# SSM front of a four-layer kernel: SiLU from the activation table, loop bodies ordered chunk by chunk

## What is computed

```
xr, gate = split(x @ W_in.T, 2)
xr = xr + t_emb[:, None, :]
xc = causal_conv(xr, W_conv, 4 taps) + b_conv
xc = silu(xc)
mu, var = xc.mean(-1), xc.var(-1)
xn = (xc - mu) / sqrt(var + 1e-05) * ln_g + ln_b
Bm, Cm, dt = split(xn @ W_xproj.T, 3)
dt = tanh(dt @ W_dt.T + b_dt) * 0.01
Ad = 1.0 + dt * -tanh(A_log)
Bd = Bm * minimum(norm(xn), 1.0)
h = clip(h * ad + bd * xt, -10, 10); y_t = c_t . h       (scan over the 64 tokens)
out = (y + D * xn) * silu(gate) @ W_out.T
```

## Time and profile before

| | us |
|---|---|
| median of 3 runs | 2034.54 (2029.61 to 2037.28) |
| the profiled execution, its own time | 2042.08 |
| its span in the profile | 2040.3 |
| busy in the span: PE, DVE, ACT, POOL | 1783.1, 1706.3, 1327.3, 658.3 |

### The profile page before, as it was taken

The page is one execution under the profiler, slowest core; times in us unless marked ns, Lnnn a source line. Parts: engine busy times, 40 slices in busy tenths (PEclk is TensorE's granted clock), DMA queues, the critical chain, the costliest instruction groups (busy, mean ns, idle before and its releaser), DMA issues.

```text
span 2040.3 us, 46458 instructions
## 1 busy us (share of the span) xinstructions
PE 1783.1 (87%) x15152; PEld 853.0 (42%) x15152; DVE 1706.3 (84%) x2508; ACT 1327.3 (65%) x2180; POOL 658.3 (32%) x592
## 2 busy tenths in 40 slices
PE   7899898998988787788998997987787889899978
PEld 5555455555544545442222223444454322222234
DVE  4778878787776898989999996668888899999965
ACT  4545445454443778698998992048776899899910
POOL 0233223332222011434765660001014356656500
PEclk9999999999998898979999999999998899999999
DMA  3000000000000333354554746712333545546477
GB/s 145 2 2 0 1 2 28 2 1 0 1 2 32 121 110 138 109 180 135 175 160 123 248 145 212 219 50 104 129 129 118 173 138 173 159 155 225 145 220 270
DMA packets 127179, 228.29 MB, mean 112 GB/s; under 512 B 36084, under 2 KB 61812, under 8 KB 118004
## 3 DMA queue, kind: packets, MB, share of 16 engines
q1 hardware_dynamic: 127064, 226.80, 34.1%
HBM read 143.40 MB, written 83.36 MB: 111 GB/s over the span
## 4 chain that ended last, share of the span: by engine, by line
PE 57%; DVE 18%; ACT 11%; issue 7%; DMA 4%; SPq 2%; DVEq 0%; ACTq 0%; POOL 0%; POOLq 0%
PE PS L1237 12%; PE PS L1254 12%; PE PS L1095 9%; PE PS L881 8%; DMA yt<-y_d 3%; DVE q L1669 3%; ACT ex L653 3%; DVE ex L1371 3%; PE PS L1257 3%; PE PS L1304 2%; PE PS L1148 2%; PE PS L947 2%; DVE sm L1377 2%; DVE mx L1367 2%; DVE z L1557 2%
## 5 line engine op out<-in xcount | busy, mean ns | idle before, releaser
L866 ACT ACTIVATE R<-q,Ast 128x512 f32<-128x512 f32 x1024 | 637.7, 709 | 42.3 <-DVE q L1669 29.6
L1669 DVE SCALAR_TENSOR_TENSOR q<-R,PS 128x512 f32<-128x512 f32 x1008 | 612.0, 705 | 20.4 <-PE PS L1237 10.1
L548 POOL TENSOR_TENSOR Uw<-Ub,rowmask 96x512 bf16<-96x512 bf16 x256 | 338.9, 1357 | 193.9 <-PE PS L1237 181.3
L1237 PE MATMUL PS<-xq,Uw 97*128 97x512 bf16 x1024 | 323.7, 394 | 53.4 <-DVE q L1669 39.3
L1254 PE MATMUL PS<-q,Wy 128*32 128x512 f32 x2016 | 284.7, 618 | 0.8 <-DVE q L1669 0.7
L539 POOL TENSOR_TENSOR xlo<-xr,xmi 128x512 bf16<-128x512 f32 x64 | 72.3, 1161 | 529.3 <-ACT xmi L791 529.3
L1237 PEld LDWEIGHTS PS<-xq,Uw 97*128 97x128 bf16 x1024 | 85.7, 97 | 366.6 <-DVE q L1669 321.2
L1095 PE MATMUL PS<-X,Win 128*128 (+1 forms) x512 | 232.0, 603 | 4.3 <-DVEq L1501 2.9
L881 PE MATMUL PS<-xn,Wl 128*128 128x512 f32 x384 | 185.4, 614 | 25.8 <-DVE xm L1347 19.0
L505 POOL TENSOR_TENSOR ex<-ex,rs 128x1024 f32<-128x1024 f32 x32 | 94.1, 2941 | 206.1 <-DVE rs L1380 206.1
L649 ACT ACTIVATE pT<-PS 128x512 f32<-128x512 f32 x128 | 75.3, 596 | 119.1 <-PE PS L947 118.9
(11 more groups left out here) (151 smaller groups left out, 2744.5 us busy)
## 6 DMA issues: line engine op xcount, KB each, us to landing
xq<-xpart_d SPq DMA_DIRECT2D x384, 192.0 KB
sg_d<-sg SPq DMA_DIRECT2D x16, 1024.0 KB, 4.2
xn_d<-z SPq DMA_DIRECT2D x16, 1024.0 KB, 4.0
y_d<-ys SPq DMA_DIRECT2D x64, 256.0 KB, 3.9
xnp<-xn_d SPq DMA_DIRECT2D x16, 1024.0 KB, 6.6
sgp<-sg_d SPq DMA_DIRECT2D x16, 1024.0 KB, 9.1
yt<-y_d SPq DMA_DIRECT2D x32, 512.0 KB, 10.0
xpart_d<-xh SPq DMA_DIRECT2D x16, 512.0 KB, 2.9
```

Of the source, the lines that this page charges most:

```text
L548: pl.tensor_tensor(Uw[0:XROWS, h, w, :, :, :], Ub[0:XROWS, w, 0:N, ds(s0, CH)].rearrange("p n t -> p t n").unsqueeze(2).broadcast_to([XROW ...
L866: act.activation(R[:, w, :], q[:, t % 2, w, :], ACT.Relu, scale=Ast[:, h, w, t:t + 1], bias=CLIP).then_inc(ac_r, 1)
L1237: pe.matmul(PS[:, w, :], Uw[0:KROWS, h, w, t, :, :].rearrange("p b n -> p (b n)"), xq[0:KROWS, hb, w, s8 % XT, :], start=True, stop=True). ...
L1669: v.scalar_tensor_tensor(out=q[:, s8 % 2, w, :], in0=R[:, w, :], scalar=2 * CLIP, in1=PS[:, w, :], op0=ALU.min, op1=ALU.subtract).then_inc ...
```

## The change

```diff
-LN_EXP_SET = 6
+LN_EXP_SET, SILU_TANH_SET = 6, 18
...
+            def silu_set():
+
+                act.add_instruction(mybir.InstLoadActFuncSet(name=nc.get_next_instruction_name(), act_func_set_id=SILU_TANH_SET))
...
+                silu_set()
                 act.activation(tA[:, :], dtp[:, 1:2], ACT.Tanh).then_inc(tA_r, 1)
...
-                def gate_tanh(n):
-                    for m in range(DC):
-                        act.wait_ge(g_mm, n * DC + m + 1)
-                        act.wait_ge(z_r, n * DC + m + 1)
-                        act.activation(th[:, m, :], PS[:, m, :], ACT.Tanh, scale=0.5).then_inc(sgt_r, 1)
-
-                def conv_tanh(n):
-                    for m in range(DC):
-                        act.wait_ge(cv_r, n * (3 * DC) + 2 * DC + m + 1)
-                        act.activation(th[:, m, :], acc[:, m, :], ACT.Tanh, scale=0.5).then_inc(th_r, 1)
...
+                def conv_silu(n, m):
+                    act.wait_ge(cv_r[2], n * DC + m + 1)
+                    act.activation(zs[:, m, :], acc[:, m, :], ACT.Silu).then_inc(z_r, 1)
+
+                def gate_silu(n, m):
+                    act.wait_ge(sg_st, n * 16 + 16)
+                    act.wait_ge(g_mm, n * DC + m + 1)
+                    act.activation(sg[:, m, :], PS[:, m, :], ACT.Silu).then_inc(sg_r, 1)
...
                 def decay_in(it):
+                    act.wait_ge(xd_mm, it + 1)
+                    act.activation(dts[:, :], PS[:, 6, 2 * P:3 * P], ACT.Copy).then_inc(dts_r, 1)
+
+                def minus_c(it):
                     act.wait_ge(xw_mm, it + 1)
-                    act.activation(dts[:, :], PS[:, 6, 2 * P:3 * P], ACT.Copy).then_inc(dts_r, 1)
                     act.wait_ge(pick_st, it * PICK + PICK)
                     act.activation(Cn[:, :], PS[:, 6, P:2 * P], ACT.Copy, scale=-1.0).then_inc(C_r, 1)
...
                 def body(it):
-                    logarithm_set()
-                    tap(it + 1)
                     log_std(it, 4)
-                    for m in range(DC):
-                        shifted(it, m)
-                    for m in range(DC):
-                        squared(it, m)
-                    conv_tanh(it + 1)
-                    gate_tanh(it + 1)
+                    silu_set()
+                    tap(it + 1, 0)
+                    tap(it + 1, 1)
+                    tap(it + 1, 2)
+                    gate_silu(it + 1, 0)
+                    shifted(it, 0)
+                    shifted(it, 1)
+                    squared(it, 0)
+                    gate_silu(it + 1, 1)
+                    shifted(it, 2)
+                    shifted(it, 3)
+                    tap(it + 1, 3)
+                    gate_silu(it + 1, 2)
+                    squared(it, 1)
+                    squared(it, 2)
                     decay_in(it)
+                    conv_silu(it + 1, 0)
+                    squared(it, 3)
+                    high_part(it, 0, 0)
                     decay_tanh(it, PS[:, 4, 0:P])
+                    conv_silu(it + 1, 1)
+                    high_part(it, 1, 1)
+                    gate_silu(it + 1, 3)
+                    conv_silu(it + 1, 2)
+                    conv_silu(it + 1, 3)
                     logarithm_set()
                     log_norm(it)
-                    for k in range(TT):
-                        high_part(it, k, k)
                     mean(it + 1)
-                    for k in range(TT):
-                        middle_part(it, k)
-                    squares(it + 1)
-
-                tap(l * G)
-                conv_tanh(l * G)
-                gate_tanh(l * G)
+                    minus_c(it)
+                    high_part(it, 2, 2)
+                    middle_part(it, 0)
+                    high_part(it, 3, 3)
+                    middle_part(it, 1)
+                    for m in range(DC):
+                        square(it + 1, m)
+                    middle_part(it, 2)
+                    middle_part(it, 3)
+
+                for m in range(DC):
+                    tap(l * G, m)
+                for m in range(DC):
+                    conv_silu(l * G, m)
+                for m in range(DC):
+                    gate_silu(l * G, m)
                 mean(l * G)
-                squares(l * G)
+                logarithm_set()
+                for m in range(DC):
+                    square(l * G, m)
                 with act.Fori(0, G - 1) as g:
                     body(l * G + g)
-                logarithm_set()
                 log_std(l * G + G - 1, 6)
...
+                def x_in_proj(it, g, m):
+                    pe.wait_ge(xr1_r, it * TT + m + 1)
+                    into(it + 1, g + 1, m, xr_mm)
+
+                def turned_x(it, k):
+                    pe.wait_ge(sg_r, (it + 1) * DC + k + 1)
+                    turn_x(it, k, k)
+
                 def body(it, g):
-                    for m in range(DC):
-                        pe.wait_ge(sg_r, it * DC + m + 1)
-                        pe.wait_ge(xr1_r, it * TT + m + 1)
-                        into(it + 1, g + 1, m, xr_mm)
-                    variance(it, 4)
-                    gates(it + 1, g + 1, 0, DC - 1)
+                    x_in_proj(it, g, 0)
+                    variance(it, 0, 4)
+                    x_in_proj(it, g, 1)
+                    variance(it, 1, 4)
+                    variance(it, 2, 4)
+                    variance(it, 3, 4)
+                    x_in_proj(it, g, 2)
+                    gate_in(it + 1, g + 1, 0)
                     pe.wait_ge(zr_r, it * 3 + 3)
                     spread_out(5, zr, zb_mm)
-                    gates(it + 1, g + 1, DC - 1, DC)
-                    project_part(it, 2)
-                    project_part(it, 0)
-                    project_part(it, 1, xw_mm)
-                    norm(it)
-                    for k in range(TT):
-                        pe.wait_ge(sg_r, (it + 1) * DC + k + 1)
-                        turn_x(it, k, k)
-                        if k == 0:
-                            decay(it, PS[:, 4, 0:P])
+                    gate_in(it + 1, g + 1, 1)
+                    x_in_proj(it, g, 3)
+                    gate_in(it + 1, g + 1, 2)
+                    norm(it, 0)
+                    project_part(it, 2, xd_mm)
+                    turned_x(it, 0)
+                    turned_x(it, 1)
+                    decay(it, PS[:, 4, 0:P])
+                    gate_in(it + 1, g + 1, 3)
                     pe.wait_ge(dtt_r, it + 1)
-                    mean(it + 1)
+                    mean(it + 1, 0)
+                    norm(it, 1)
+                    mean(it + 1, 1)
+                    norm(it, 2)
+                    turned_x(it, 2)
+                    norm(it, 3)
+                    mean(it + 1, 2)
+                    mean(it + 1, 3)
+                    project_part(it, 1)
+                    project_part(it, 0, xw_mm)
+                    turned_x(it, 3)
                     pe.wait_ge(mu_r, it + 2)
                     spread_out(5, mus, zm_mm)
                     fold_b(it)
...
-                def silu(n):
-                    for m in range(DC):
-                        v.wait_ge(th_r, n * DC + m + 1)
-                        v.scalar_tensor_tensor(out=zs[:, m, :], in0=th[:, m, :], scalar=1.0, in1=acc[:, m, :],
-                                               op0=ALU.add, op1=ALU.mult).then_inc(z_r, 1)
-
-                def gate(n):
-                    v.wait_ge(sg_st, n * 16 + 16)
-                    for m in range(DC):
-                        v.wait_ge(sgt_r, n * DC + m + 1)
-                        v.scalar_tensor_tensor(out=sg[:, m, :], in0=th[:, m, :], scalar=1.0, in1=PS[:, m, :],
-                                               op0=ALU.add, op1=ALU.mult).then_inc(sg_r, 1)
...
                 def body(it, g):
-                    embed(it + 1, g + 1)
-                    conv(it + 1, (0,))
+                    embed(it + 1, g + 1, 0)
                     inverse_std(it, 4)
-                    conv(it + 1, (1,))
+                    embed(it + 1, g + 1, 1)
+                    embed(it + 1, g + 1, 2)
+                    conv(it + 1, 0, 0)
                     for m in range(DC):
                         gained(it, m, 5)
-                    conv(it + 1, (2,))
-                    silu(it + 1)
-                    gate(it + 1)
+                    conv(it + 1, 1, 0)
+                    embed(it + 1, g + 1, 3)
+                    conv(it + 1, 0, 1)
+                    conv(it + 1, 0, 2)
+                    conv(it + 1, 1, 1)
+                    conv(it + 1, 2, 0)
+                    conv(it + 1, 1, 2)
+                    conv(it + 1, 2, 1)
+                    conv(it + 1, 0, 3)
+                    conv(it + 1, 1, 3)
+                    conv(it + 1, 2, 2)
+                    conv(it + 1, 2, 3)
+                    decay(it)
+                    rest(it, 0, 0)
                     norm_bound(it)
-                    decay(it)
+                    over(it)
```

(57 more changed lines are left out.)

92 lines of the change are left out of this document (39 added, 53 removed).

## The result

The changed kernel takes 1968.93 us (median of 4 runs, 1968.33 to 1975.12); the kernel before took 2035.91 us beside it (2029.61 to 2038.41). The ratio is 0.9682, with a 95% interval of 0.9652 to 0.9712: 67 us shorter. Predicted were 1949 us: 1934 to 1963 as the forecast's own range, widened to 1980 by the rivals. The time lies in the widened range and outside the forecast's own. The profiled executions differ by 2040.3 - 1966.5 = 73.8 us of span.

A forecast was written before the change was run, and what follows sets the result against it. The bound was taken as DVE's length plus its waits for ACT. Terms 94 - 11 + 5 - 2.4 = 86 us gave 1956, and 1949 us as the runs' median; own range 1934 to 1963, with rivals to 1980.

The forecast's parts named there:

- The subtraction (25.55): Front's loop body: 32.52 us less 4.81 of DVE's removed steps and 2.16 of its tanh wait gives 25.55 us.
- the layout: Front's loop body laid out by hand in both orders with the trace's durations: old 32.1 us, new 25.1 us.
- The body, 94 us: SSM front: each of 14 loop bodies falls by 6.7 us to 25.8 us, 94 us in all.
- Silu at the tanh's price: ACT's eight Silus a body cost what the tanhs did, 616 and 587 ns.
- The rivals of the drain: ACT also stops 1.28 us before each table load: body 27 us, kernel 1964 us; chance 0.05.
- the clock: PE still runs 4 us of each body at half clock: body 27.2 us, kernel about 1967 us; chance 0.06.
- the dear Silu: ACT's Silus cost more than tanhs; at 2.0 us each, body 34.4 us and kernel 2061 us; chance 0.03.
- The engines hand on badly: Three nearly full engines in strict order let delays through: body 28 us, kernel 1977 us; chance 0.16.
- The tables, -11 us: DVE stops 5.5 us once a layer for the `xn` store behind the scan's table loads: 11 us lost.
- Uw beside the taps, nothing: Seventh body: DVE's taps meet POOL's `Uw` as before; nothing counted, within 3 us either way a layer.
- First group +5: First group, nothing overlapped: the gate's four DVE steps before `z` go, 5 us gained for two layers.
- the last `zs` -2.4: Front's end: SP waits for the last `zs`, now after `sg`, by two Silus: 2.4 us lost.

The follow-up runs named there:

- the last kernel: Changed kernel with DVE operands out of PSUM, SP's stores ahead of the tables, and PE's fold of B behind the next group's first input projection: 1932.82 us.

## Why the prediction was right, and where it was off

The sign, the place and the kinds of effect were right, and the time is within the stated range. Of the 86 us, 67 came. That is outside the forecast's own 1934 to 1963, and the body of 26.93 us misses the 25 to 26.5 that were to show it: the range held because it took in times that were put down to rivals.

- **The bound.** "The body is DVE's length plus the places at which DVE waits for ACT" was wrong for the kernel before. It was set by a chain in which DVE's taps had no part: taking 4.8 us from DVE alone left the steady bodies at 32.51 us against 32.44. The subtraction (25.55) came near the layout (25.1) by luck. The layout knew the order (32.1 and 25.1), and the forecast of the body was made from it.
- **The body, 94 us.** This term is the one mis-sized. 5.59 us instead of 6.7, 14 times, is 78. Of the 1.1 us missing in a body, 0.71 are `eC` held by POOL's `xlo`, shown in two ways. The remaining 0.4 are argued, not tested: PE's stretch from the fold to the fourth `xp` takes 13.0 us in the chain, where my layout, of which no row is shown here, had 12.2. PE's work, put at 24.8 us, shows as 25.71 us busy here and as 24.91 in the last kernel.
- **Silu at the tanh's price, two table loads, no drain, PE's clock:** as stated for the steady bodies; behind the stop for the tables the clock is 0.87. The rivals of the drain, the clock and the dear Silu are out, though the first two named times (1964 and 1967) nearer to the measured one than the forecast did. "The engines hand on badly" (1977) was too dear, and DVE's waits of 1.2 us don't reach its 2.5. But its premise, that strict order lets each delay through, holds in the ring: the 0.71 us of `eC` went into the body whole.
- **The tables, -11 us.** The stop is 5.87 us, and the interval is 8.8 us over the steady ones where before it was 1.4 over; the next one is 1.3 and 2.4 us under them, hardly more than the 1.4 of before. That is 14 us for both layers instead of 11.
- **Uw beside the taps, nothing.** That interval was 5.2 and 5.7 us over the steady ones, and is 3.4 over now: 4 us for me, inside the 3 us either way for each layer.
- **First group +5, the last `zs` -2.4.** The first gate store comes 2.3 and 1.9 us earlier after the first `xp`: 4.2. From the last gate store to the 17th scan product the two layers take 2.4 and 1.9 us more. SP waits at 839.81 for `zs` as stated, and again ahead of the B stores, since `eC` and the split are late.
- **The sum.** The 14 intervals shrank by 35.3 and 33.5 us, the first groups by 4.2, and 4.3 are lost at the ends: 68.7 us in the front. The other 5 us between the profiled executions are outside it, 3.5 of them in the first layer's scan and post stages, and the medians of the runs don't show them.

## What to carry to other kernels

Follow the chain of waits once round a loop body before taking work off the fullest engine: work counted here only on the ring, and a change that took 17% off the fullest engine gave 0.2% until the order was changed as well. When an order changes, list what now runs on POOL beside each VectorE operation whose inputs both lie in SBUF. Multiply a gain for a body only by the bodies that have nothing else to wait for.

## What the hardware showed unexpectedly

- Two VectorE operations (128x126 and 128x128) with both inputs in SBUF took 291 ns alone, and 999 and 1149 ns beside POOL subtractions of 1.16 us; with one input from PSUM 289 and 291 ns beside the same work. A cast from SBUF took 228 ns alone and 824 beside it.
- PE's busy time in the profile fell from 25.54 to 24.91 us for the same 264 matmuls at the same granted clock, when one wait was taken out of their way.
- With PE relieved (24.5 us of work in 26.2), one steady interval in each layer lasted 28.7 and 28.5 us; the granted clock over the first of them was 0.94. In it PE had waited 1.72 us for `rB` up to 696.53, against 0.7 in the body before; the clock over 696 to 704 was 0.79, and four projection matmuls took 3.45 us where the next four took 1.98. `rB` was late as `mr` ahead of it was held by `xlo` for 1.30 us.
